# Two accumulation chains interleaved: the experts' first layer alternates between its two PSUM banks

## The chip, the cores and the metric

One core of a Trainium2 chip runs the whole kernel. The metric is device time in microseconds (us) of one execution, the median over several runs; lower is better. Busy times, waits and single instructions come from one profiled execution. Short names in the rows: PE is TensorE's matmul side, PEld its weight loads, DVE VectorE, ACT ScalarE, POOL GpSimd, SP the engine that issues most DMAs.

## What is computed

The program is one layer of a graph network over 6250 rows of 256 features. The layer norm of the rows feeds a graph part and a linear-attention part; their sum with the input is normalised again and goes through eight experts, weighted by a router. The change lies in the experts:

```
h = einsum('bfd,edh->bfeh', x, W1) + b1
h = relu(_bn(h, g1, be1, m1, v1))
h = einsum('bfeh,ehk->bfek', h, W2) + b2
h = relu(_bn(h, g2, be2, m2, v2))
y = einsum('bfeh,ehd->bfed', h, Wo) + bo
return einsum('bfed,fe->bfd', y, w)
```

## The kernel before, in words

The rows are cut into 13 chunks: chunk 0 has 240 rows, chunks 1 to 11 have 512, chunk 12 has 378. A first stage (to about 170 us) goes over all rows for the graph tables and the attention sums and loads the expert weights into SBUF. The rest of the time is a loop over chunks, and in each over the eight experts. Activations lie with features on the 128 partitions and rows along the free dimension, so 256 features are two halves of 128: an input half `k` and an output half `h`.

Every product keeps close to fp32 by splitting both factors into a high and a low part (`fp32r`) and adding three products: high times high, high times low, low times high. `mm3` issues them (lines 300, 301 and 302) for both input halves: six matmuls into one bank. A layer of an expert is two such groups, one for each output half: twelve matmuls, each 128x128 weights with `R` moving columns, where R is the chunk's number of rows.

The order is written out by hand on each engine. TensorE's loop for expert `e` issues L1 of expert e+1 (or of expert 0 of the next chunk), then L2 of e, then L3 of e-1, and after them some work for the next chunk. So three layers of other experts, 36 matmuls, stand between an expert's L1 and its L2, and as many between its L2 and its L3.

- `L1(ch, e)` writes banks 0 and 1 (`L1b[h]`). Each half waits until ScalarE has read the bank for the expert before (`r1`, counted by half) and raises `l1` when it is complete. In the first expert of a chunk it also waits for the low part of the turned input (`f2lo`, counted by input half).
- ScalarE: `relu1` does, for each half in turn, `relu` (line 960, from the bank to `activated`, raises `r1`) and `high1` (line 809, the high part, `h_high`). `relu2` does the same for the second layer: both `relu`s to `weight_stage`, then both high parts (`h`), which wait until L3 has read the only `h` buffer.
- VectorE: `hid1` takes the low parts (`h_low`, line 1403), which release L2; `weigh_hidden` (line 1548) multiplies by the router's weight; `hid2` takes the low parts of the second layer (`h`, line 1403), which release L3. Work for the next chunk stands between these, among it `route` (from line 1700) and `weights`.
- In chunk 0 TensorE also has `router_turn` (line 1339), which waits for VectorE's `weights`, and GpSimd issues two of chunk 1's gathers only when `h1` has reached 2 and 4, that is behind the first two experts' `hid1`.

Of the kernel before, what the change touches and what calls it, by code (L numbers as in the profile page):

```python
# [13 lines left out]
P = 128  # L14
KT = D // P
# [6 lines left out]
NE = 8  # L22
# [48 lines left out]
def need(eng, sem, value):  # L71
    if value > 0:
        eng.wait_ge(sem, value)
# [14 lines left out]
def build(nc, I, out):  # L88
    ctx = ExitStack()
    with ctx:  # L90
        def sb(name, shape, dt=fp32):
            return ctx.enter_context(nc.sbuf_tensor(name, shape, dt))

        def sem(name):
            return ctx.enter_context(nc.semaphore(name))
# [22 lines left out]
        xTh = sb("xT_high", [P, 2, KT, CH], f32r)  # L118
        xTl = sb("xT_low", [P, 2, KT, CH], f32r)
# [94 lines left out]
        L1b, L2b, Yb, Fb = bank[0:2], bank[2:4], bank[4:6], bank[6:8]  # L214
# [10 lines left out]
        s = {n: sem("s_" + n) for n in names}  # L225
# [66 lines left out]
        def mm3(dst, lhs, rhs, ready=None, first=True, final=True):  # L292

            last = None
            n = len(lhs)
            for k in range(n):
                (ah, al), (bh, bl) = lhs[k], rhs[k]
                if ready:
                    ready(k)
                nc.tensor.matmul(dst, ah, bh, start=(first and k == 0), stop=False)  # L300
                nc.tensor.matmul(dst, ah, bl, start=False, stop=False)  # L301
                last = nc.tensor.matmul(dst, al, bh, start=False, stop=(final and k == n - 1))  # L302
            return last
# [771 lines left out]
        def _(pe):  # L1075
# [24 lines left out]
            for k in range(KT):  # L1100
                need(pe, s["kv_w"], k + 1)
                for i in range(KT):
                    last = nc.tensor.matmul(KVb[2 + i][:, :], (centre if i == k else spread), wkv[:, k, :],  # L1103
                                            start=False, stop=(k == KT - 1))
# [3 lines left out]
            for k in range(KT):  # L1108
                last = nc.tensor.matmul(XTb[0][:, 0:D], onesf[:, :], wg[:, k, 0:D], start=(k == 0), stop=(k == KT - 1))
# [100 lines left out]
            for grp in range(2):  # L1210
                last = nc.tensor.matmul(KVb[1 - grp][:, 0:D], kvT[:, grp, :], w1m[:, grp, :], start=True, stop=True)
# [4 lines left out]
            for k in range(KT):  # L1216
                for grp in range(2):
                    last = nc.tensor.matmul(KVb[2 + k][:, 0:D], wqT[:, grp, k * P:(k + 1) * P], Pm[:, grp, :],
                                            start=False, stop=(grp == 1))
# [3 lines left out]
            for h in range(2):  # L1223
                for grp in range(2):
                    last = nc.tensor.matmul(XTb[0][:, h:h + 1], Pm[:, grp, h * P:(h + 1) * P], bqc[:, grp:grp + 1],
                                            start=(grp == 0), stop=(grp == 1))
# [3 lines left out]
            def W(layer, e, k, lo, hi):  # L1230
                m = layer * NE + e
                return whi[:, m, k * D + lo:k * D + hi], wlo[:, m, k * D + lo:k * D + hi]

            def L1(ch, e):
                R = ch.rows

                def turned(k):
                    need(pe, s["f2lo"], KT * ch.c + k + 1)

                for h in range(2):  # L1240
                    need(pe, s["r1"], 2 * NE * ch.c + 2 * (e - 1) + h + 1)
                    mm3(L1b[h][:, 0:R], [W(0, e, k, h * P, (h + 1) * P) for k in range(KT)],
                        [(xTh[:, ch.par, k, 0:R], xTl[:, ch.par, k, 0:R]) for k in range(KT)],
                        turned if e == 0 and h == 0 else None).then_inc(s["l1"], 1)

            def L2(ch, e):
                R = ch.rows
# [113 lines left out]
            idle(3)  # L1361
            pe.wait_ge(s["wst_lo"], len(JOBS))
            L1(CHUNKS[0], 0)
            router(CHUNKS[0])

            for ch in CHUNKS:
                nxt = None if ch.last else ch.next()
                for e in range(NE):
                    if e + 1 < NE:
                        L1(ch, e + 1)  # L1370
                    elif nxt is not None:
                        L1(nxt, 0)
                    L2(ch, e)
                    if ch.c == 0:
                        if e == 0:
                            router_turn(ch)
                        elif e == 1:
                            out_bias(ch)
                    if e > 0:
                        L3(ch, e - 1)  # L1380
                    elif ch.c > 0:
                        L3(ch.prev(), NE - 1)
                    if e == 2 and ch.c > 0:
                        out_bias(ch)
                    if ch.c == 0 and e == 2:
                        mix2(nxt)
                    elif nxt is not None and by_dma(nxt) and e == 5:
                        pass
                    elif nxt is not None and e in FRONT and not (ch.c == 0 and e == 3):
                        FRONT[e](nxt)  # L1390
# [429 lines left out]
```

## Time and profile before

| | |
|---|---|
| median of 3 runs | 1075.84 us (1074.94 to 1076.32) |
| profiled execution, its own time | 1074.75 us |
| its span, first to last instruction | 1072.9 us |
| matmuls | 5316, PE busy 1060.2 us |
| ScalarE busy | 727.1 us |
| VectorE busy | 774.4 us |
| mean granted TensorE clock | 0.998 |

The profiled execution took 1.85 us more than its span, and its time lies 1.09 us under the median. A matmul's length in the profile is longer than the distance to the next one's start, since matmuls overlap; the distance between starts is what a matmul costs when the stream is dense. Starts are printed to 0.01 us.

### The profile page before, as it was taken

The page shows a single profiled execution, that of the slowest core. Times are in us where ns is not written, and L with a number is a line of the kernel's source. Part 1 is how long each engine was busy: PE and PEld are TensorE (multiplying, and loading weights), DVE is VectorE, ACT ScalarE, POOL GpSimd, SP SyncE. Part 2 cuts the span into 40 slices and gives each one's busy share as a digit, 9 for nine tenths or more (in the row PEclk, how much of TensorE's full clock was granted, in tenths as well). Part 3 has the DMA queues.
Part 4 walks back from the last instruction along what each step waited for, and adds up shares of the span by engine and source line. Part 5 has one row for each costly group of instructions (what it writes and reads, how often), then busy time and mean ns, then how long its engine had stood idle before and what let it go on. Part 6 is the DMA issues. An engine that isn't in the chain of part 4 may idle for free.

```text
span 1072.9 us, 16901 instructions
## 1 busy us (share of the span) xinstructions
PE 1060.2 (99%) x5316; PEld 899.0 (84%) x5316; DVE 774.4 (72%) x1644; ACT 727.1 (68%) x1263; POOL 279.6 (26%) x308
## 2 busy tenths in 40 slices
PE   9999998999999999999999999999999999999997
PEld 7998987988888888888888888888888888888897
DVE  8888756868686686776866867768768668676664
ACT  5777756676775766757757767667667576675674
POOL 4787764303023022130130321211302202110010
PEclk9999999999999999999999999999999999999999
DMA  6877852244154244441641443325416423341030
GB/s 193 267 232 250 246 176 61 81 112 120 23 141 117 72 82 109 110 107 46 142 115 46 113 109 99 88 75 124 118 23 145 115 82 65 93 112 26 3 95 15
DMA packets 235439, 116.55 MB, mean 109 GB/s; under 512 B 170932, under 2 KB 217918, under 8 KB 235350
## 3 DMA queue, kind: packets, MB, share of 16 engines
q1 hardware_dynamic: 229070, 107.94, 37.8%
q0 software_dynamic: 3968, 6.71, 2.4%
q10 hardware_dynamic: 2311, 0.84, 0.3%
q8 instruction: 42, 0.69, 0.3%
q14 instruction: 48, 0.39, 0.1%
HBM read 77.46 MB, written 37.97 MB: 108 GB/s over the span
## 4 chain that ended last, share of the span: by engine, by line
PE 93%; DVE 2%; issue 2%; POOL 1%; DMA 1%; ACT 1%; SPq 0%; POOLq 0%; DVEq 0%; ACTq 0%
PE bank L300 29%; PE bank L301 29%; PE bank L302 29%; PE bank L1146 2%; PE bank L1333 1%; PE bank L1087 1%; PE bank L1351 1%; PE bank L1079 1%; POOL gathered L751 0%; POOL alpha_l L753 0%; PE bank L1103 0%; DMA expert_weight_rows<-expert_weights 0%; DMA expert_weights<-router_w_blocks 0%; DVE h_low L1403 0%; ACT activated L960 0%
## 5 line engine op out<-in xcount | busy, mean ns | idle before, releaser
L809 ACT ACTIVATE h<-weight_stage 128x512 fp32r<-128x512 f32 (+2 forms) x206 | 117.7, 603 | 191.5 <-PE bank L302 108.8
L1403 DVE TENSOR_TENSOR h_low<-activated,h_high 128x512 fp32r<-128x512 f32 (+2 forms) x208 | 136.3, 666 | 93.7 <-ACT h_high L809 91.2
L1403 DVE TENSOR_TENSOR h<-weight_stage,h 128x512 fp32r<-128x512 f32 (+2 forms) x206 | 126.8, 657 | 80.3 <-ACT h L809 80.3
L960 ACT ACTIVATE activated<-bank,bn_cols 128x512 f32<-128x512 f32 (+2 forms) x208 | 154.6, 743 | 39.4 <-PE bank L302 37.7
L960 ACT ACTIVATE weight_stage<-bank,bn_cols 128x512 f32<-128x512 f32 (+2 forms) x208 | 149.7, 745 | 21.6 <-PE bank L302 21.1
L300 PE MATMUL bank<-h_high,ffn_w_high 128*128 128x512 f32 (+2 forms) x420 | 158.1, 376 | 0.1
L301 PE MATMUL bank<-h_low,ffn_w_high 128*128 128x512 f32 (+2 forms) x420 | 157.8, 376 | 0.0
L302 PE MATMUL bank<-h_high,ffn_w_low 128*128 128x512 f32 (+2 forms) x420 | 157.8, 376 | 0.0
L300 PE MATMUL bank<-xT_high,ffn_w_high 128*128 128x512 f32 (+2 forms) x416 | 157.1, 378 | 0.1
L301 PE MATMUL bank<-xT_low,ffn_w_high 128*128 128x512 f32 (+2 forms) x416 | 156.7, 377 | 0.0
L302 PE MATMUL bank<-xT_high,ffn_w_low 128*128 128x512 f32 (+2 forms) x416 | 156.5, 376 | 0.0
L300 PE MATMUL bank<-h,ffn_w_high 128*128 128x512 f32 (+1 forms) x380 | 146.4, 385 | 0.9 <-DVE h L1403 0.9
L302 PE MATMUL bank<-h,ffn_w_low 128*128 128x512 f32 (+1 forms) x380 | 146.4, 385 | 0.0
L301 PE MATMUL bank<-h,ffn_w_high 128*128 128x512 f32 (+1 forms) x380 | 146.4, 385 | 0.0
L778 POOL TENSOR_TENSOR accumulated<-accumulated,normalised 128x512 f32<-128x512 f32 x22 | 37.8, 1741 | 393.2 <-DVE normalised L1557 393.2
L809 ACT ACTIVATE h_high<-activated 128x512 fp32r<-128x512 f32 (+2 forms) x208 | 126.1, 606 | 6.6
L300 PEld LDWEIGHTS bank<-h_high,ffn_w_high 128*128 128x128 f32 x420 | 78.9, 188 | 14.7 <-DVE h_low L1403 0.5
L302 PEld LDWEIGHTS bank<-h_high,ffn_w_low 128*128 128x128 f32 x420 | 79.0, 188 | 13.7
L301 PEld LDWEIGHTS bank<-h_low,ffn_w_high 128*128 128x128 f32 x420 | 78.9, 188 | 13.7
L300 PEld LDWEIGHTS bank<-xT_high,ffn_w_high 128*128 128x128 f32 x416 | 78.2, 188 | 14.0 <-issue 0.5
L302 PEld LDWEIGHTS bank<-xT_high,ffn_w_low 128*128 128x128 f32 x416 | 78.2, 188 | 14.0
L301 PEld LDWEIGHTS bank<-xT_low,ffn_w_high 128*128 128x128 f32 x416 | 78.2, 188 | 13.4
(244 smaller groups left out, 1992.8 us busy)
## 6 DMA issues: line engine op xcount, KB each, us to landing
expert_weight_rows<-expert_weights SPq DMA_DIRECT2D x44, 256.0 KB, 3.9
x_rows<-in_x SPq DMA_DIRECT2D x18, 512.0 KB, 4.8
x_turned<-xT_high SPq DMA_DIRECT2D x22, 256.0 KB, 3.4
x_turned<-xT_low SPq DMA_DIRECT2D x22, 256.0 KB, 4.6
x_rows<-accumulated SPq DMA_DIRECT2D x11, 512.0 KB
x_rows<-expert_weights SPq DMA_DIRECT2D x22, 256.0 KB, 6.0
accumulated<-x_rows SPq DMA_DIRECT2D x88, 64.0 KB
out<-accumulated SPq DMA_DIRECT2D x88, 64.0 KB, 1.9
```

Source lines behind the costliest of these rows:

```text
L300: nc.tensor.matmul(dst, ah, bh, start=(first and k == 0), stop=False)
L301: nc.tensor.matmul(dst, ah, bl, start=False, stop=False)
L302: last = nc.tensor.matmul(dst, al, bh, start=False, stop=(final and k == n - 1))
L778: nc.gpsimd.tensor_tensor(x2b[:, h, 0:w], x2b[:, h, 0:w], yblk[:, h, 0:w], ALU.add).then_inc(s["fin"], 1)
L809: return nc.scalar.activation(dst, src, ACT.Copy)
L960: nc.scalar.activation(dst[:, h, 0:ch.rows], src[h][:, 0:ch.rows], ACT.Relu, bias=bnp[:, 1, layer, col:col + 1], scale=bnp[:, 0, layer, co ...
L1079: nc.tensor.matmul(XTb[1][:, 0:P], onesf[:, :], onesf[:, :], start=True, stop=True)
L1087: last = nc.tensor.transpose(Tb[:, k, i * T.tp:(i + 1) * T.tp], xn[0:T.tp, T.slot, k * P:(k + 1) * P], ident[0:T.tp, 0:T.tp])
L1146: last = nc.tensor.matmul(Sb[:, grp * P:(grp + 1) * P], kvn[0:tp, p, vc], kvn[0:tp, p, kc], start=False, stop=final, skip_group_check=True)
L1333: last = nc.tensor.matmul(Fb[0][:, 0:ch.rows], wr4[:, i % KT, :], part, start=(i == 0), stop=(i == len(parts) - 1))
L1351: nc.tensor.matmul(Yb[h][:, 0:ch.rows], bo3[0:3 * NE, 0, h * P:(h + 1) * P], wT[:, 0:ch.rows], start=False, stop=False).then_inc(s["fbo"], 1)
L1403: return V.tensor_tensor(dst, full, high.bitcast(fp32), ALU.subtract)
```

## The change

In `L1` the two groups of six become one loop. The input half is the outer loop, the three products the middle one, and the output half the inner one. Each piece of the moving operand (high or low part of one input half) is thus streamed twice in succession, with another 128x128 weight tile and into the other bank. The order of the three products changes too: high weights with high rows, low weights with high rows, high weights with low rows. The number of matmuls and of weight loads, their shapes, and all work of the other engines stay as they are.

```
-                for h in range(2):
-                    need(pe, s["r1"], 2 * NE * ch.c + 2 * (e - 1) + h + 1)
-                    mm3(L1b[h][:, 0:R], [W(0, e, k, h * P, (h + 1) * P) for k in range(KT)],
-                        [(xTh[:, ch.par, k, 0:R], xTl[:, ch.par, k, 0:R]) for k in range(KT)],
-                        turned if e == 0 and h == 0 else None).then_inc(s["l1"], 1)
+                for k in range(KT):
+                    xh, xl = xTh[:, ch.par, k, 0:R], xTl[:, ch.par, k, 0:R]
+                    if e == 0:
+                        turned(k)
+                    for step in range(3):
+                        for h in range(2):
+                            if k == 0 and step == 0:
+                                need(pe, s["r1"], 2 * NE * ch.c + 2 * (e - 1) + h + 1)
+                            wh, wl = W(0, e, k, h * P, (h + 1) * P)
+                            last = nc.tensor.matmul(L1b[h][:, 0:R], (wh, wl, wh)[step], (xh, xh, xl)[step],
+                                                    start=(k == 0 and step == 0), stop=(k == KT - 1 and step == 2))
+                            if k == KT - 1 and step == 2:
+                                last.then_inc(s["l1"], 1)
```

TensorE's rows for L1 of expert 1 in chunk 0, before. Bank 0 and bank 1 are the two output halves; a row ends with the semaphores that the instruction waits for.

```order
L300 MATMUL bank0<-xT_high,ffn_w_high 128x240 [waits s_r1]
L301 MATMUL bank0<-xT_low,ffn_w_high 128x240
L302 MATMUL bank0<-xT_high,ffn_w_low 128x240
L300 MATMUL bank0<-xT_high,ffn_w_high 128x240
L301 MATMUL bank0<-xT_low,ffn_w_high 128x240
L302 MATMUL bank0<-xT_high,ffn_w_low 128x240
L300 MATMUL bank1<-xT_high,ffn_w_high 128x240 [waits s_r1]
L301 MATMUL bank1<-xT_low,ffn_w_high 128x240
L302 MATMUL bank1<-xT_high,ffn_w_low 128x240
L300 MATMUL bank1<-xT_high,ffn_w_high 128x240
L301 MATMUL bank1<-xT_low,ffn_w_high 128x240
L302 MATMUL bank1<-xT_high,ffn_w_low 128x240
```

Bank 0 is complete with the sixth matmul, and the second wait stands on the seventh. The same place in the changed kernel:

```order
L1249 MATMUL bank0<-xT_high,ffn_w_high 128x240 [waits s_r1]
L1249 MATMUL bank1<-xT_high,ffn_w_high 128x240 [waits s_r1]
L1249 MATMUL bank0<-xT_high,ffn_w_low 128x240
L1249 MATMUL bank1<-xT_high,ffn_w_low 128x240
L1249 MATMUL bank0<-xT_low,ffn_w_high 128x240
L1249 MATMUL bank1<-xT_low,ffn_w_high 128x240
L1249 MATMUL bank0<-xT_high,ffn_w_high 128x240
L1249 MATMUL bank1<-xT_high,ffn_w_high 128x240
L1249 MATMUL bank0<-xT_high,ffn_w_low 128x240
L1249 MATMUL bank1<-xT_high,ffn_w_low 128x240
L1249 MATMUL bank0<-xT_low,ffn_w_high 128x240
L1249 MATMUL bank1<-xT_low,ffn_w_high 128x240
```

Bank 0 is now complete with the eleventh matmul, bank 1 with the twelfth as before, and the wait for bank 1 stands on the second matmul. Every other L1 moves in the same way; in chunks 1 to 11 its rows read 128x512.

## Rows read from the trace of the kernel before

**Rows 1.** The page, part 1: busy time, share of the span, instructions

```profile
PE 1060.2 (99%) x5316; PEld 899.0 (84%) x5316; DVE 774.4 (72%) x1644; ACT 727.1 (68%) x1263; POOL 279.6 (26%) x308
```

**Rows 2.** The page, part 4: chain that ended last, by engine

```profile
PE 93%; DVE 2%; issue 2%; POOL 1%; DMA 1%; ACT 1%; SPq 0%; POOLq 0%; DVEq 0%; ACTq 0%
```

**Rows 3.** TensorE's waits from 170 us on: total us, times, longest

```profile
PE bank L1339 <- DVE router_w L1399: 1.6, 1, 1.6
...
PE bank L300 <- DVE h L1403: 1.3, 2, 0.9
```

**Rows 4.** Windows: stretch, us, busy by engine, TensorE clock, DMA share, GB/s

```profile
280.40:353.10 72.70, 72.70 (x332) 60.12 (x331) 52.72 (x104) 49.22 (x76) 14.00 (x13) 1.00 0.38 96
```

**Rows 5.** Timeline of PE, chunk 7, L1 of expert 5: start, us

```profile
693.76 0.39 PE L302 MATMUL bank<-xT_high,ffn_w_low 128*128 128x512 f32 x1
693.99 0.39 PE L300 MATMUL bank<-xT_high,ffn_w_high 128*128 128x512 f32 x1
...
695.35 0.39 PE L300 MATMUL bank<-h_high,ffn_w_high 128*128 128x512 f32 x1
...
700.79 0.39 PE L300 MATMUL bank<-xT_high,ffn_w_high 128*128 128x512 f32 x1
```

**Rows 6.** Timeline of PE in the set-up, lines 1103 and 1109

```profile
8.83 3.60 PE L1103 MATMUL bank<-activated,gathered 128*128 128x512 f32 x8
12.27 0.59 PE L1109 MATMUL bank<-weight_stage,ones 128*128 128x256 f32 x2
```

**Rows 7.** Timeline of PE, chunk 0, from L1 of expert 0

```profile
174.56 0.27 PE L302 MATMUL bank<-xT_high,ffn_w_low 128*128 128x240 f32 x1
...
175.12 0.27 PE L301 MATMUL bank<-xT_low,ffn_w_high 128*128 128x240 f32 x1
...
175.79 0.27 PE L300 MATMUL bank<-xT_high,ffn_w_high 128*128 128x240 f32 x1
...
177.37 0.38 PE L300 MATMUL bank<-h_high,ffn_w_high 128*128 128x240 f32 x1
...
180.57 0.29 PE L1339 MATMUL bank<-identity,router_w 120*64 120x120 f32 x1 [1.60 <-DVE router_w L1399]
```

**Rows 8.** Timeline of ACT, chunk 0, expert 0

```profile
174.87 0.56 ACT L960 ACTIVATE activated<-bank,bn_cols 128x240 f32<-128x240 f32 x1 [0.23 <-PE bank L302]
...
175.77 0.54 ACT L960 ACTIVATE activated<-bank,bn_cols 128x240 f32<-128x240 f32 x1
176.34 0.40 ACT L809 ACTIVATE h_high<-activated 128x240 fp32r<-128x240 f32 x1
```

**Rows 9.** Timeline of DVE, chunk 0, expert 0 and the router

```profile
176.59 0.72 DVE L1403 TENSOR_TENSOR h_low<-activated,h_high 128x240 fp32r<-128x240 f32 x2
177.23 1.02 DVE L1700 STREAM_TRANSPOSE router_w<-bank 32x64 f32<-32x64 f32 x4
```

**Rows 10.** Timeline of ACT, chunk 1, expert 2, second half

```profile
233.54 0.76 ACT L960 ACTIVATE activated<-bank,bn_cols 128x512 f32<-128x512 f32 x1
```

**Rows 11.** Timeline of PE, chunk 1, start of L1 of expert 3

```profile
233.40 0.39 PE L300 MATMUL bank<-xT_high,ffn_w_high 128*128 128x512 f32 x1
233.63 0.39 PE L301 MATMUL bank<-xT_low,ffn_w_high 128*128 128x512 f32 x1
```

**Rows 12.** Chain of work around a wait of PE: start, us, what

```profile
230.46 0.14 issue
230.59 0.47 PE bank L300
```

**Rows 13.** Timeline of ACT, chunk 7, expert 5, first half

```profile
694.19 0.78 ACT L960 ACTIVATE activated<-bank,bn_cols 128x512 f32<-128x512 f32 x1 [3.06 <-PE bank L302]
```

**Rows 14.** Chunk 9: ACT's second half of expert 0, PE's L1 of expert 1

```profile
796.29 0.77 ACT L960 ACTIVATE activated<-bank,bn_cols 128x512 f32<-128x512 f32 x1
...
798.95 0.39 PE L300 MATMUL bank<-xT_high,ffn_w_high 128*128 128x512 f32 x1
```

**Rows 15.** Timeline of ACT, chunk 12, second layer of expert 6

```profile
1060.94 0.52 ACT L809 ACTIVATE h<-weight_stage 128x378 fp32r<-128x378 f32 x1 [1.46 <-PE bank L302]
```

## The prediction, written before the changed kernel ran

> **What bounds the kernel now.** I read the busy times first: PE is busy for 99% of the span, ScalarE for 68%, VectorE for 72% [rows 1]. A busy PE alone proves little, so I read the chain of waits next: 93% of it is PE [rows 2]. The list of TensorE's waits then has only 4.4 us from 170 us on, in four waits, all at 172 to 231 us; the two groups of them that matter here are shown [rows 3]. One whole chunk of 512 rows (72.7 us) has PE busy throughout at a granted clock of 1.00 [rows 4]. So from chunk 2 on, the time is the number of matmuls times the distance between their starts, and the change can act in two ways only: by altering that distance, or by making TensorE wait where it did not.
>
> **The distance between starts.** In L1 of a chunk with 512 rows, the last six matmuls go from 693.99 to 695.35: 0.227 us each [rows 5]. 512 columns at 2.4 GHz take 0.213 us, so about 13 ns of each matmul is not streaming. If that were the price of adding twice in a row into one bank, a matmul that starts another bank would be cheaper. The trace before has such pairs: the sixth matmul of L1 ends the work on bank 0 and the seventh opens bank 1, at 693.76 and 693.99, 0.23 us apart [rows 5]. The twelfth to L2's first changes bank, rows and weights, and is no nearer. Hence I cost the alternation at nothing.
>
> The other new property, the same rows streamed twice in succession into two banks, has one likeness in the set-up: line 1103 multiplies each input half with two weight tiles into banks 2 and 3, twice over (eight records). They take (12.27 - 8.83) / 8 = 0.430 us each [rows 6]. These are plain fp32, two passes of 512 columns for each record, so 0.427 us is pure streaming. Here too a repeated stream is neither faster nor slower. I take 0.227 us after the change. The bounds are: if the whole 13 ns went away in all of L1's 1248 matmuls (13 chunks by 8 experts by 12), 16.6 us less; if a bank change cost as much again, 16.6 us more. The rows of before stand at the zero between these ends.
>
> The Trainium skill (TensorE: Matmul & The Clock Gate, the section "Wait — 56ns, not 53.3ns?") gives a warm matmul about 2.5 ns over its streaming time. This trace differs: it has 13 ns for these fp32r matmuls. If the new order brought L1 to the page's figure, an estimate from the page is 1248 x 11 ns = 14 us less; by the trace's own bank changes it is nothing.
>
> **What becomes late.** The first bank is complete with the eleventh matmul instead of the sixth: 5 x 0.227 = 1.13 us later in the large chunks, 5 x 0.112 = 0.56 us in chunk 0. The second bank is complete when it was. ScalarE's `relu` of the first half can start 0.43 us after the start of the bank's last matmul (694.19 against 693.76, [rows 5, 13]). I went along all 104 experts. In 47 ScalarE starts less than 1 us after the bank is due and shifts by most of this, up to 1.13 us; in the others it is already late with other work, and loses less or nothing. The two halves of ScalarE's work follow each other without a gap, so all of `relu1` shifts, then VectorE's `h_low`, and `relu2` behind it.
>
> In chunks 1 to 12 that lateness is covered. Between an expert's L1 and its L2 stand 36 matmuls of other layers, 36 x 0.227 = 8.2 us, and the next L1 starts 6.6 us after the `relu` that waited (694.19 to 700.79, [rows 5, 13]). The tightest release of a next L1 after chunk 1 is in chunk 9: ScalarE has read bank 1 at 796.29 + 0.77 = 797.06, the next L1 starts at 798.95, 1.89 us later [rows 14]; and there `relu` waits for the router's exponential, not for the bank, so nothing shifts. In chunk 12, with 378 columns for 512, the lateness is about 0.85 us, and ScalarE sits idle for 1.46 us before the high parts of the second layer [rows 15]. Those high parts wait for L3's reading of the `h` buffer, a TensorE time. So the end is not touched either.
>
> **Term 1, chunk 0, expert 0: +0.42 us.** Here there is no cover. `relu` starts at 174.87, 0.31 us after the sixth matmul's start at 174.56. The eleventh starts at 175.12, so it would be 175.43 [rows 7, 8]. The second half's high part goes from 176.34 to 176.90 and ends at 177.30. VectorE's second `h_low` can then start at about 177.33 and takes 0.40, to 177.73; now the pair ends at 176.59 + 0.72 = 177.31 [rows 9]. So `route` behind it is 0.42 us late, then the router's weights, for which TensorE waits 1.6 us at line 1339 [rows 3, 7], and the gathers that GpSimd issues after `h_low`. I find no slack that takes it up.
>
> **Term 2, the early wait in chunk 0: 0.** L1 of expert 1 starts at 175.79 [rows 7]. Its second matmul now needs ScalarE's second read, which ends at 175.77 + 0.54 + 0.56 = 176.87 [rows 8]. With 0.14 us from a release to the matmul (seen at 230.59, [rows 12]) it goes at 177.01, the twelfth near 178.2, and L2 at 178.3 instead of 177.37. L2 then ends at about 179.7, still before the router's release at 180.57 + 0.42. The wait of 1.6 us hides it. Were that cover gone, it would cost some 0.9 us.
>
> **Term 3, the early wait in chunk 1: +0.8 us.** L1 of expert 3 starts at 233.40 and its second matmul at 233.63 [rows 11]. ScalarE, late after the wait for the first expert weights, reads bank 1 for expert 2 only at 233.54 to 234.30 [rows 10]. Before, the wait stood on the seventh matmul (234.76) and was met. Now it stands on the second, which goes at 234.30 + 0.14 = 234.44 instead of 233.63: 0.81 us. The chain gives the first matmul after such a wait 0.47 us at 230.59 [rows 12], so some 0.1 us of restart may come on top; I leave it to the range. Behind this point PE has no wait that could absorb it. Bounds: 0 if ScalarE is earlier in another run, 1.1 us if the wake-up is slower.
>
> **Sum.** 0.42 + 0 + 0.81 = +1.2 us. Span 1072.9 becomes 1074.1; with the 1.85 us outside it, 1075.95 against the profiled 1074.75. Put on the median of the runs, 1075.84 + 1.2 = 1077.0 us, or 0.11% more. A difference under 0.2% (2.15 us) can't be told from none, so my verdict is "the same".
>
> **Rivals.**
>
> (a) The distance shrinks. For it speaks the unexplained 13 ns; against it the bank changes at full distance and the repeated streams of line 1103. Those are not the same thing as twelve alternations in fp32r, so I leave it a chance. At full effect 1077.0 - 16.6 = 1060.4 us; at a third of it 1071.5. It decides from 3 ns for each matmul on. 8%.
>
> (b) Slower through waits in every chunk. The lateness of 1.13 us also moves VectorE, and with it the turned rows of the next chunk, which travel through DRAM. If one release in each of chunks 1 to 12 ran out of slack by 0.5 us, the sum is 6 us: 1083. It decides from 0.07 us a chunk. Against it: the tightest gap that I found after chunk 1 is 1.89 us. 10%.
>
> (c) The distance grows, because two open chains or a repeated stream cost something that a single change of bank does not show. 3 ns each make 3.7 us: 1080.7. 4%.
>
> (d) The clock. L1 in one chunk with the clock at its lower level would cost 12 x 0.227 = 2.7 us for each expert. Against it: the six banks 0 to 5 are already gone through in turn at a granted clock of 1.00 [rows 4], and the only new idle time is under 1.2 us at a stretch. The Trainium skill (TensorE: Matmul & The Clock Gate, "A second HAM failure mode: psum-queue depth-cycling") says that cycling through banks can leave small idle gaps that make the clock swing. One expert's L1 at half rate is 1077.0 + 2.7 = 1079.7 us. 3%.
>
> (e) The change does as above: 75%, of which a few in a hundred fall past either bound by the scatter of the runs (the three shown span 1.4 us).
>
> **The numbers.** Faster by over 0.2% (under 1073.7): 8% from (a) and 1% of (e). Slower by over 0.2% (over 1078.0): 17% from (b), (c), (d) and 2% of (e), since my sum already leans that way. The same: 72%. The range takes in the scatter of 0.7 us to each side, both ends of term 3, and the small halves of (a) and (b): 1074.3 to 1079.3.
>
> **What the profile after would show.** The distance of L1's starts at 0.227 us. `relu` of the first half 0.43 us after the eleventh matmul. A gap of about 0.8 us beyond the usual distance between the first and second matmul of L1 of expert 3 in chunk 1, and one of about 1.1 us in expert 1 of chunk 0, with the wait at the router's turn shortened. No further TensorE waits after 240 us, and every chunk of 72.7 us. A chunk that is more than 0.1 us off that would make the prediction wrong; so would a distance other than 0.227.

## The result, and the profile after

The changed kernel takes 1077.62 us (median of 19 runs, 1076.88 to 1079.87) beside 1075.84 us for the kernel before (19 runs of the same session, 1074.44 to 1077.44). The ratio is 1.0019, with a 95% interval of 1.0012 to 1.0026, so +2.0 us (1.3 to 2.8); the two medians by themselves lie 1.78 us apart. That is just inside the 0.2% that stood for "the same". The profiled execution took 1078.52 us with a span of 1076.7 us, 3.8 us more span than before. The page after, busy times and then the chain by engine:

```profile
PE 1062.4 (99%) x5316; PEld 900.3 (84%) x5316; DVE 773.2 (72%) x1644; ACT 723.5 (67%) x1263; POOL 273.7 (25%) x308
...
PE 94%; issue 1%; POOL 1%; DVE 1%; ACT 1%; DMA 1%; SPq 0%; POOLq 0%; ACTq 0%; DVEq 0%
```

The counts are those of [rows 1], and TensorE is the chain as in [rows 2]. TensorE's waits from 170 us on (us in total, times, longest):

```profile
PE bank L1249 <- ACT activated L960: 1.6, 3, 0.6
PE bank L300 <- DVE h L1411: 1.6, 2, 1.2
PE bank L1333 <- DVE normalised L1681: 1.5, 1, 1.5
PE bank L1347 <- DVE router_w L1407: 1.2, 1, 1.2
```

The first row is new: three waits for ScalarE in the changed loop, at line 1249. The last answers to the 1.6 us at line 1339 in [rows 3] and is 0.4 us shorter. All lie ahead of 240 us. Two chunks of 512 rows, in windows as in [rows 4]:

```profile
284.50:357.23 72.73, 72.73 (x331) 60.16 (x330) 53.19 (x105) 48.98 (x76) 13.36 (x13) 1.00 0.39 96
357.23:429.96 72.73, 72.73 (x331) 60.16 (x330) 51.76 (x104) 48.70 (x76) 13.47 (x13) 1.00 0.39 97
```

TensorE is busy from end to end at a granted clock of 1.00. Measured from the first router matmul of one chunk to that of the next, each of the chunks 2 to 10 takes 72.73 us in both kernels. Inside the L1 groups of chunks 2 to 11, the mean distance between starts is 227.2 ns before and 227.2 ns after (880 distances each). TensorE's timeline at the place of [rows 5], the end of L1 of expert 5 in chunk 7 and L2's first:

```profile
698.68 0.61 PE L1249 MATMUL bank<-xT_low,ffn_w_high 128*128 128x512 f32 x2
699.13 0.39 PE L300 MATMUL bank<-h_high,ffn_w_high 128*128 128x512 f32 x1
```

The first row holds the eleventh and twelfth matmul, bank 0's last and bank 1's last. ScalarE's timeline beside it:

```profile
699.11 0.78 ACT L960 ACTIVATE activated<-bank,bn_cols 128x512 f32<-128x512 f32 x1 [4.19 <-PE bank L1249]
```

ScalarE reads bank 0 0.43 us after the eleventh matmul's start, the same delay as in [rows 5, 13] (694.19 against 693.76); its idle time ahead of that grew from 3.06 to 4.19 us, by the 1.13 us of five matmuls. None of that reaches TensorE.

So the loss lies in chunks 0 and 1. In chunk 0, ScalarE's timeline after:

```profile
176.78 0.55 ACT L960 ACTIVATE activated<-bank,bn_cols 128x240 f32<-128x240 f32 x1 [0.79 <-PE bank L1249]
177.36 0.40 ACT L809 ACTIVATE h_high<-activated 128x240 fp32r<-128x240 f32 x1
177.67 0.53 ACT L960 ACTIVATE activated<-bank,bn_cols 128x240 f32<-128x240 f32 x1
178.23 0.40 ACT L809 ACTIVATE h_high<-activated 128x240 fp32r<-128x240 f32 x1
```

VectorE's:

```profile
177.94 0.40 DVE L1411 TENSOR_TENSOR h_low<-activated,h_high 128x240 fp32r<-128x240 f32 x1
178.67 0.41 DVE L1411 TENSOR_TENSOR h_low<-activated,h_high 128x240 fp32r<-128x240 f32 x1 [0.33 <-ACT h_high L809]
179.00 1.02 DVE L1708 STREAM_TRANSPOSE router_w<-bank 32x64 f32<-32x64 f32 x4
```

And TensorE's in chunk 0, then in chunk 1 (L1 of expert 1, then of expert 3):

```profile
177.38 0.38 PE L1249 MATMUL bank<-xT_high,ffn_w_high 128*128 128x240 f32 x1
178.25 0.38 PE L1249 MATMUL bank<-xT_high,ffn_w_high 128*128 128x240 f32 x1 [0.49 <-ACT activated L960]
179.59 0.27 PE L300 MATMUL bank<-h_high,ffn_w_high 128*128 128x240 f32 x1
...
182.34 0.29 PE L1347 MATMUL bank<-identity,router_w 120*64 120x120 f32 x1 [1.25 <-DVE router_w L1407]
...
218.94 0.40 PE L1249 MATMUL bank<-xT_high,ffn_w_high 128*128 128x512 f32 x1
219.84 0.50 PE L1249 MATMUL bank<-xT_high,ffn_w_high 128*128 128x512 f32 x1 [0.51 <-ACT activated L960]
220.19 0.64 PE L1249 MATMUL bank<-xT_high,ffn_w_low 128*128 128x512 f32 x2
...
236.31 0.39 PE L1249 MATMUL bank<-xT_high,ffn_w_high 128*128 128x512 f32 x1
237.26 0.50 PE L1249 MATMUL bank<-xT_high,ffn_w_high 128*128 128x512 f32 x1 [0.56 <-ACT activated L960]
237.60 0.63 PE L1249 MATMUL bank<-xT_high,ffn_w_low 128*128 128x512 f32 x2
```

Chunk 0's first L1 matmul is at 175.27 here and at 173.92 before. TensorE's timelines, before and after:

```profile
173.92 0.35 PE L300 MATMUL bank<-xT_high,ffn_w_high 128*128 128x240 f32 x1
...
175.27 0.35 PE L1249 MATMUL bank<-xT_high,ffn_w_high 128*128 128x240 f32 x1
```

Counted from there, the router's transpose on VectorE starts at +3.73 (179.00 - 175.27) against +3.31 (177.23 - 173.92, [rows 9]), 0.42 us later, and the released router matmul at +7.07 against +6.65 (180.57 - 173.92, [rows 7]), again 0.42. Expert 1's wait in chunk 0 (178.25) ends far ahead of that and costs nothing. In chunk 1 the wait of expert 3 is the predicted one. The wait of expert 1 at 219.84 was not predicted.

The span's 3.8 us divide so. 1.35 us lie ahead of chunk 0's first L1 matmul, in code that the change does not touch. From there to the last matmul it is 893.07 us before and 895.50 after, 2.43 more: chunk 0 has 35.85 for 35.37 (+0.48), chunk 1 has 71.96 for 70.00 (+1.96), the rest is equal.

### The profile page after: what moved, and what is told of

Same layout as the page of the kernel before. It is cut to its first block, busy times and chain, and to the rows that moved or that the text cites. A ratio compares the mean times of both kernels' runs of the same rounds, so it can differ in the third digit from the quotient of the medians.

```text
span 1076.7 us, 16901 instructions
## 1 busy us (share of the span) xinstructions
PE 1062.4 (99%) x5316; PEld 900.3 (84%) x5316; DVE 773.2 (72%) x1644; ACT 723.5 (67%) x1263; POOL 273.7 (25%) x308
## 4 chain that ended last, share of the span: by engine, by line
PE 94%; issue 1%; POOL 1%; DVE 1%; ACT 1%; DMA 1%; SPq 0%; POOLq 0%; ACTq 0%; DVEq 0%
PE bank L1249 24%; PE bank L300 21%; PE bank L302 21%; PE bank L301 21%; PE bank L1146 2%; PE bank L1341 1%; PE bank L1087 1%; PE bank L1359 1%; PE bank L1079 1%; POOL gathered L751 0%; ACT activated L960 0%; POOL alpha_l L753 0%; PE bank L1103 0%; DMA expert_weight_rows<-expert_weights 0%; DMA expert_weights<-router_w_blocks 0%
## 5 line engine op out<-in xcount | busy, mean ns | idle before, releaser
L960 ACT ACTIVATE weight_stage<-bank,bn_cols 128x512 f32<-128x512 f32 (+2 forms) x208 | 143.5, 740 | 0.9 <-remote 0.4
L1249 PE MATMUL bank<-xT_high,ffn_w_high 128*128 128x512 f32 (+2 forms) x416 | 124.3, 379 | 1.8 <-ACT activated L960 1.6
L1249 PE MATMUL bank<-xT_high,ffn_w_low 128*128 128x512 f32 (+2 forms) x416 | 122.8, 376 | 0.0
L1249 PE MATMUL bank<-xT_low,ffn_w_high 128*128 128x512 f32 (+2 forms) x416 | 122.8, 376 | 0.0
L1249 PEld LDWEIGHTS bank<-xT_high,ffn_w_high 128*128 128x128 f32 x416 | 75.9, 188 | 16.2 <-ACT activated L960 2.8
```

Of the source, the lines that this page charges most:

```text
L960: nc.scalar.activation(dst[:, h, 0:ch.rows], src[h][:, 0:ch.rows], ACT.Relu, bias=bnp[:, 1, layer, col:col + 1], scale=bnp[:, 0, layer, co ...
L1249: last = nc.tensor.matmul(L1b[h][:, 0:R], (wh, wl, wh)[step], (xh, xh, xl)[step], start=(k == 0 and step == 0), stop=(k == KT - 1 and step ...
```

## The experiments

Each run has one profile. In the sessions of the experiments the kernel before has a median of 1075.00 us (beside the first four) and 1074.83 us (beside the next four). Three stretches are compared below: chunk 0 (its first router matmul to chunk 1's), chunk 1 (to chunk 2's), and chunk 1 without the distance between the two starts around the wait for the first expert's hidden layer near 230 us (line 300 waiting for `h`). That distance is 0.75 to 1.72 us, kernels of either order lie on both sides of 1.2, and it would hide effects of this size. The ratios of whole times can't tell these kernels apart: those without either loss have 1.0007 and 1.0006, those with one of them 1.0006 and 1.0012, and the intervals overlap. Where the loss sits is read from the stretches.

**The changed kernel again.** No edit; what repeats of the 2.0 us, and where?

> The changed kernel once more, for a second profile and a tighter interval. Theory (waits at the start): ratio 1.001 to 1.0025; from L1 of expert 0 in chunk 0 on, the profile is 1.3 to 2.5 us longer than before, all of it ahead of chunk 2, chunks 2 to 11 at 72.73 us each. In the first profile ScalarE stood idle for 2.1 us at 209.5 us with nothing late for it, and TensorE then waited 0.7 us in L1 of expert 1 in chunk 1. If that pause is chance, it is gone here, and the part of chunk 1 falls to about 1.1 us (expert 3's wait of 0.8 us and what follows); if the change brings it, it is there again. Rival (the first stage before 170 us got longer by 1.4 us through the change): the first L1 starts at about 175.3 us again instead of 173.9.

Measured: 1076.19 us, ratio 1.0012 (1.0003 to 1.0021); from the first L1 matmul on 894.46 us, 1.4 more than before. Chunk 0 is 35.79 us; chunk 1 without the wait near 230 us is 69.58, for 68.71 before. Every chunk from 2 on is as before. The first L1 starts at 174.76 us. Over all twelve profiles that start lies between 173.84 and 176.60 us, and it is 174.66 in the second profile of the kernel before; so nothing shows that the change made the first stage longer. Its timeline of TensorE has the wait in L1 of expert 3 again, and none in expert 1:

```profile
235.72 0.50 PE L1249 MATMUL bank<-xT_high,ffn_w_high 128*128 128x512 f32 x1 [0.53 <-ACT activated L960]
236.06 0.62 PE L1249 MATMUL bank<-xT_high,ffn_w_low 128*128 128x512 f32 x2
```

**The old order in chunks 0 and 1.** The alternation stays in chunks 2 to 12, eleven thirteenths of it:

```
+                if ch.c < 2:
+                    for h in range(2):
+                        need(pe, s["r1"], 2 * NE * ch.c + 2 * (e - 1) + h + 1)
+                        mm3(L1b[h][:, 0:R], [W(0, e, k, h * P, (h + 1) * P) for k in range(KT)],
+                            [(xTh[:, ch.par, k, 0:R], xTl[:, ch.par, k, 0:R]) for k in range(KT)],
+                            turned if e == 0 and h == 0 else None).then_inc(s["l1"], 1)
+                    return
```

> L1 alternates in chunks 2 to 12 only; chunks 0 and 1 have the old order. Theory (all of the loss is in chunks 0 and 1): ratio to before 1.0000, within 0.0007; no TensorE wait at L1. Rival (the alternation costs in every chunk by waits or distance): ratio stays near 1.0018.

Measured: 1075.31 us, ratio 1.0007 (0.9998 to 1.0016), span 1072.8. From the first L1 matmul on 892.69 us, for 893.07 before. TensorE's waits from 170 us on:

```profile
PE bank L1354 <- DVE router_w L1414: 1.6, 1, 1.6
PE bank L1340 <- DVE normalised L1688: 1.5, 1, 1.5
PE bank L300 <- DVE h L1418: 0.8, 2, 0.4
```

No wait for ScalarE's reading is left, and the router's is back at 1.6 us. So in chunks 2 to 12 the alternation costs and gives nothing in the trace. The ratio lies at the edge of what was expected, and its interval includes 1.

**The old order in chunk 1 alone** (`ch.c == 1` in the same edit).

> Alternating except in chunk 1. Theory: only term 1 is left, 0.4 to 0.5 us, ratio 1.0004; no wait at L1 of experts 1 and 3 in chunk 1. Rival (the loss is in the steady chunks or in the first stage): ratio 1.0018.

Measured: 1075.47 us, ratio 1.0006 (0.9997 to 1.0015). Chunk 0 has 35.67 us, 0.30 more than before where 0.4 to 0.5 was expected; chunk 1 without the wait near 230 us is 68.71, exactly the value before. TensorE's waits:

```profile
PE bank L1340 <- DVE normalised L1688: 1.5, 1, 1.5
PE bank L1354 <- DVE router_w L1414: 1.2, 1, 1.2
PE bank L300 <- DVE h L1418: 0.7, 2, 0.4
PE bank L1256 <- ACT activated L960: 0.5, 1, 0.5
```

The last is chunk 0's hidden wait, and the router's wait is the shorter one of 1.2 us.

**The old order in chunk 0 alone** (`ch.c == 0`).

> Alternating except in chunk 0. Theory: term 1 is gone, the early wait of expert 3 in chunk 1 is left: 0.8 to 1.1 us, ratio 1.0009; 1.5 us (1.0014) if expert 1 of chunk 1 waits as well. Rival (the loss comes from chunk 0, whose lateness is carried on into chunk 1): ratio 1.0002 or less.

Measured: 1075.99 us, ratio 1.0012 (1.0003 to 1.0021). The opposite picture: chunk 0 is 35.28 us, chunk 1 without the wait near 230 us 69.59. TensorE's timeline in chunk 1:

```profile
230.43 0.47 PE L300 MATMUL bank<-h,ffn_w_high 128*128 128x512 f32 x1 [0.55 <-DVE h L1418]
...
234.18 0.50 PE L1256 MATMUL bank<-xT_high,ffn_w_high 128*128 128x512 f32 x1 [0.55 <-ACT activated L960]
```

With TensorE held up by only 0.55 us at 230.43, the wait in expert 3 is as long as in the other kernels. Each loss is there without the other.

**Only two of the 104 L1 in the old order**, expert 0 of chunk 0 and expert 3 of chunk 1 (`(ch.c, e) in ((0, 0), (1, 3))`).

> All of the 104 groups of L1 alternate but two: expert 0 of chunk 0 and expert 3 of chunk 1 have the old order. Theory (the loss sits in these two places: the late first bank and the early wait): ratio 1.0000 to 1.0004; the stretch from router to router of chunk 0 is 35.4 us and that of chunk 1 within 0.3 us of what its wait for the expert weights (near 230 us, 0.4 to 1.2 us in the profiles so far) makes of it, with no wait at L1 of expert 3. Rival (each alternating group of chunks 0 and 1 costs a little): the loss falls by no more than a tenth, ratio 1.0011.

Measured: 1075.53 us beside 1074.83, ratio 1.0006 (0.9997 to 1.0015). Chunk 0 is 35.45, chunk 1 without the wait near 230 us 68.67. TensorE's timeline there:

```profile
231.26 0.47 PE L300 MATMUL bank<-h,ffn_w_high 128*128 128x512 f32 x1 [1.13 <-DVE h L1418]
...
234.06 0.39 PE L300 MATMUL bank<-xT_high,ffn_w_high 128*128 128x512 f32 x1
234.29 0.39 PE L301 MATMUL bank<-xT_low,ffn_w_high 128*128 128x512 f32 x1
```

The wait is gone, with 102 of 104 experts still alternating, and the stretches are back at their lengths of before: in each of the two chunks the loss hangs on one L1. The ratio of the whole time is over the 1.0004 that was expected; its interval includes 1.

**Bank 0 three matmuls ahead.** Three into bank 0, six alternating, three into bank 1, so that bank 0 is complete with the ninth and bank 1 is opened by the fourth:

```
+                order = ([(0, 0, step) for step in range(3)] +
+                         [t for step in range(3) for t in ((1, 0, step), (0, 1, step))] +
+                         [(1, 1, step) for step in range(3)])
+                for h, k, step in order:
...
+                    if k == 0 and step == 0:
+                        need(pe, s["r1"], 2 * NE * ch.c + 2 * (e - 1) + h + 1)
```

> Every L1: three products of bank 0, then six that alternate between bank 1 and bank 0, then three of bank 1. No rows stream twice in succession. Bank 0 is complete with the ninth matmul, and the second wait stands on the fourth. Theory by the same two terms: bank 0 is 3 x 0.112 = 0.34 us late in chunk 0, of which 0.14 us is idle time of VectorE that takes it up, so +0.20 us; in chunk 1 the fourth matmul of expert 3 is due at 234.08 on the clock of before and goes at 234.44, +0.36 us and 0.1 us of restart. Sum 0.6 to 0.7 us, ratio 1.0006; the gap in L1 of expert 3 is 0.6 us instead of 0.92. Rival (alternation as such costs at the start, wherever the wait stands): 1.3 us as in the changed kernel.

Measured: 1075.82 us, ratio 1.0007 (0.9998 to 1.0016). Chunk 1 without the wait near 230 us is 69.10: +0.4 for the +0.9 of the full alternation. Chunk 0 is 35.44, only +0.1 where +0.2 was expected. The distance of starts from chunk 2 on is again 227.2 ns. TensorE's timeline in L1 of expert 3:

```profile
236.25 0.39 PE L1250 MATMUL bank<-xT_low,ffn_w_high 128*128 128x512 f32 x1
236.71 0.73 PE L1250 MATMUL bank<-xT_high,ffn_w_high 128*128 128x512 f32 x2
```

The fourth matmul follows the third at 0.46 us in place of 0.23; 0.6 was expected. The loss shrinks with the number of matmuls between L1's start and the second wait. That the wait comes early is what counts here: six of the twelve matmuls still alternate.

**Bank 0 later still, 12 matmuls.** The changed kernel makes bank 0 late by five matmuls. A wait in ScalarE's `relu`, from chunk 2 on and not for expert 0, makes that twelve: it holds the read of bank 0 until the first half of L2 is through, the 18th matmul counted from L1's first, where the kernel before has the bank ready with the sixth. That is up to 12 x 0.227 = 2.72 us:

```
+                if layer == 0 and ch.c >= 2 and e > 0:
+                    need(act, s["l2"], 2 * NE * ch.c + 2 * (e - 1) + 1)
```

> The changed kernel, and from chunk 2 on ScalarE's read of the first layer waits in experts 1 to 7 for the first half of the L2 that follows on TensorE as well: bank 0 is read after the 18th matmul instead of the 11th, 2.72 us later than before the change, 2.4 times its lateness. It prices the cover. Theory (1.89 us or more of slack wherever ScalarE waits for nothing else, mostly 4): no or little loss on top of the changed kernel, at most 0.3 us a chunk; chunks 2 to 11 at 72.73 to 73.0 us; ratio 1.0012 to 1.004. Rival (the slack is used up soon after the 1.13 us of the change): over 0.5 us a chunk, ratio above 1.006.

Measured: 1076.71 us, ratio 1.0019 (1.0010 to 1.0028); the changed kernel had 1.0019 and 1.0012 in its two comparisons. Two of its chunks in windows:

```profile
283.06:355.79 72.73, 72.73 (x332) 60.17 (x330) 51.40 (x103) 48.41 (x75) 13.41 (x13) 1.00 0.38 96
355.79:428.52 72.73, 72.73 (x331) 60.17 (x330) 52.17 (x104) 48.43 (x76) 13.36 (x13) 1.00 0.38 97
```

Still 72.73 us, and no wait of TensorE after 240 us; only the end of chunk 12 is 0.3 us later. That the delay took hold is seen in chunk 7's expert 5. TensorE's timeline, L2's sixth matmul:

```profile
698.82 0.39 PE L302 MATMUL bank<-h_high,ffn_w_low 128*128 128x512 f32 x1
```

And ScalarE's:

```profile
699.30 0.78 ACT L962 ACTIVATE activated<-bank,bn_cols 128x512 f32<-128x512 f32 x1 [5.47 <-PE bank L302]
```

ScalarE reads bank 0 only behind that matmul, after 5.47 us of idle time for the 4.19 of the changed kernel and the 3.06 of [rows 13]. The cover in the large chunks is at least this big.

**Bank 0 later by 18 matmuls.** The same wait with `+ 2` in place of `+ 1`, so for both halves of L2, 4.1 us.

> As the run before, but waiting for both halves of that L2: bank 0 is read after the 24th matmul, 4.08 us later than before the change. Theory: the next L1 starts 8.2 us after this one and both reads take 2.1 us after 5.6 us, so 0.4 us is left in a plain expert and nothing where VectorE or ScalarE have work for the next chunk: waits of TensorE appear in a few experts of each chunk, 1 to 4 us a chunk, ratio 1.01 to 1.04. If the chunks stay at 72.73 us here too, the cover is larger than I read from the timeline.

Measured: 1083.12 us, ratio 1.0077 (1.0063 to 1.0090), +8.3 us. Windows of two chunks:

```profile
283.81:356.99 73.18, 73.04 (x331) 60.08 (x331) 51.28 (x103) 47.85 (x74) 12.69 (x13) 1.00 0.38 96
356.99:430.46 73.47, 73.32 (x331) 59.92 (x331) 51.91 (x104) 48.48 (x76) 12.79 (x13) 1.00 0.37 96
```

Now each chunk from 2 to 10 is 73.1 to 73.6 us, 0.4 to 0.9 more, and the last stretch is 1.5 us longer. That is less than the 1 to 4 us a chunk and the ratio of 1.01 or more that were expected: the cover was again read too small. But it has an edge, between 2.7 and 4.1 us of lateness. This is how rival (b) would have looked in a profile; nothing of it is in the changed kernel's.

**One more profile of each kernel**, before and changed.

> The kernel before once more, one look, for what varies between profiles of the same program. Expected: chunk 0 from router to router 35.37 us within 0.05; chunk 1 69.5 to 70.5 us, by its wait for the expert weights near 230 us; chunks 2 to 10 at 72.73 us; the first L1 anywhere from 173.8 to 176.6 us.

> The changed kernel a third time, one look. Theory: chunk 0 at 35.8 us; chunk 1 at 70.5 to 71.2 us, or near 72.0 us if ScalarE makes its pause near 210 us again (seen in one of two profiles of this program and perhaps in one of its kin). Rival (the pause belongs to the changed program): it is there again.

Measured: before again 1075.43 us, span 1073.6, chunk 0 at 35.34, chunk 1 without the wait near 230 us 68.74; changed again 1076.22 us (before beside it 1075.12), span 1074.4, chunk 0 at 35.72, chunk 1 likewise 69.60. With that wait, chunk 1 is 69.95 and 70.48 us, as expected to 0.02.

Sums over all profiles. Chunk 0 with expert 0 in the old order is 35.28 to 35.45 us in five kernels, before and its repeat among them (mean 35.37); with expert 0 alternating in full 35.67 to 35.85 in six (mean 35.78): +0.41. Chunk 1 without the wait near 230 us is 68.67 to 68.79 with expert 3 in the old order, in five kernels (mean 68.72). Alternating, it is 69.53 to 69.60 in four (mean 69.58), +0.85. In the two that are left, the changed kernel's first profile and the one with 12 matmuls of lateness, it is 70.38 and 70.25.

## Why the prediction was right, point by point

**The distance between starts** stayed at 227.2 ns (rivals (a) and (c) fall). Neither the alternation of banks nor the repeated stream of rows buys or costs anything that this trace can show. The prediction had closed its bounds of 16.6 us to none from a single bank change at 0.23 us; over the 80 L1 groups of chunks 2 to 11 before, that change from the sixth to the seventh matmul takes 227.0 ns. The Trainium skill (TensorE: Matmul & The Clock Gate, "Wait — 56ns, not 53.3ns?") puts a warm matmul about 2.5 ns over its streaming time; here the 13 ns stay in either order.

**What becomes late.** Bank 0 was late by five matmuls, and ScalarE waited for it 1.13 us longer in the place shown. In the chunks from 2 on that cost nothing. The argument by the next release was right, and cautious: a lateness of up to 2.72 us was covered too, and only six matmuls more took 0.4 to 0.9 us a chunk. Rival (b) was the right mechanism for a larger lateness, and falls for this one. The prediction's count of 47 experts takes the sixth matmul's start as the time when the bank is due; counted from 0.43 us behind it, when ScalarE could first read, it is 74. Nothing in the sum hangs on it.

**Term 1** was 0.42 by the rows and is 0.42 in the changed kernel's own rows, +0.41 over eleven profiles. **Term 2** was hidden as said: L2 began at 179.59, the released router matmul came at 182.34, and its wait shrank from 1.6 to 1.25 us. The gap ahead of the second matmul of expert 1 is 0.87 us, so 0.76 beyond the usual distance and not 1.1: the prediction let that L1 start on time, but its first matmul waits for ScalarE's late read of bank 0 (over at 176.78 + 0.55 = 177.33, matmul at 177.38).

**Term 3** was put at 0.81, with some 0.1 of restart left to the range. In the changed kernel the distance is 0.95 us for 0.227, +0.72, and the next one is 0.34, +0.11: 0.83 us together. Over the profiles the chunk grows by 0.85. That 0.81 comes so near is partly luck. The prediction took 0.14 us from the release to the matmul, from a wait for VectorE; here, where ScalarE releases, it is 0.05 (its read ends at 219.03 + 0.76 = 219.79, the matmul starts at 219.84, and the same holds for the wait at 237.26). The 0.09 too much stood in for the 0.11 of restart that was left out. The mechanism is as forecast, a wait that moved from the seventh matmul to the second and was met in the old place; the order with three matmuls of lead, which halved it, and the kernel with two old L1, which removed it, show that.

**The sum** of +1.2 us stands against +2.0 (1.3 to 2.8) in the main comparison, and +1.3 (0.3 to 2.3) in the repeat. The two terms as measured give 0.41 + 0.85 = 1.26 us. What the sum missed sits in the first profile of the changed kernel as a second stall in chunk 1, of 0.79 us (70.38 for a mean of 69.59 in the repeats). No term and no rival of the prediction has it. Its first condition stood in the profile before: in chunk 1, ScalarE's second read for expert 0 ended only 0.26 us ahead of L1 of expert 1 (216.08 + 0.76 = 216.84 against 217.10).

```profile
216.08 0.76 ACT L960 ACTIVATE activated<-bank,bn_cols 128x512 f32<-128x512 f32 x1
...
217.10 0.40 PE L300 MATMUL bank<-xT_high,ffn_w_high 128*128 128x512 f32 x1
```

With the wait on the second matmul, that leaves ScalarE 0.26 + 0.23 - 0.05 = 0.44 us to be late in. It was later than that, and the changed kernel's ScalarE timeline leads up to it:

```profile
211.64 0.55 ACT L960 ACTIVATE activated<-bank,bn_cols 128x240 f32<-128x240 f32 x1 [2.11 <-remote]
...
217.70 0.76 ACT L960 ACTIVATE activated<-bank,bn_cols 128x512 f32<-128x512 f32 x1
...
219.03 0.76 ACT L960 ACTIVATE activated<-bank,bn_cols 128x512 f32<-128x512 f32 x1
```

ScalarE was idle for 2.1 us before it read bank 0 of chunk 0's expert 7, although the eleventh matmul had started at 209.59. It was therefore late with expert 0 of chunk 1, whose second half it reads at 219.03, and the second matmul of expert 1's L1 had to wait until 219.84. The repeat of the same kernel has this at the same place:

```profile
209.32 0.55 ACT L960 ACTIVATE activated<-bank,bn_cols 128x240 f32<-128x240 f32 x1 [0.38 <-PE bank L1249]
```

There it is 0.4 us of idle, which is the plain wait for the bank: `relu` starts 0.32 us after the eleventh matmul's start (209.00), where [rows 7, 8] have 0.31 after the sixth. No wait comes in expert 1. The trace also records when each semaphore is raised. Eight profiles have chunk 0's expert 7 in one of the new orders; for them, at this place (us):

| kernel | ScalarE idle before `relu` | `l1` raised, after the start of bank 0's last matmul | wait in expert 1 of chunk 1 |
|---|---|---|---|
| changed, two repeats | 0.38 | 0.29 | none |
| chunk 1 old | 0.38 | 0.29 | (old order) |
| three matmuls of lead | 0.53 | 0.67 | none |
| two old L1 | 1.27 | 1.19 | none |
| 18 matmuls later (chunks 0 and 1 as changed) | 1.29 | 1.20 | none |
| 12 matmuls later (chunks 0 and 1 as changed) | 2.03 | 1.94 | yes |
| changed, first profile | 2.11 | 2.02 | yes |

With chunk 0 in the old order, in four profiles, ScalarE has no idle time there at all. So where the pause is long, the early second wait turns it into a stall of TensorE.

By these records it is TensorE's signal that came late, not its matmuls: `relu` starts 0.02 to 0.03 us after `l1` goes up each time. In the first profile of the changed kernel the four signals for the two halves of this L1 and of the L2 behind it come within 0.19 us, at 211.61 to 211.80, while the matmuls go on at 0.11 us each; VectorE's signals in that time come with the ends of its instructions. Why the signals came late is open. Some semaphore records just ahead of the pause are missing, so the trace is not whole there. Whether the new order brings this or the profiles of the old order just met none can't be told from eight against four. It is also open how much of the 2.0 us in the main comparison is this stall, and how much is the first stage, whose length differs by up to 2.8 us between profiles.

**The clock** (rival (d)) was 1.00 in every window with the bank changing at each matmul. The Trainium skill's warning (same page, "A second HAM failure mode: psum-queue depth-cycling") speaks of idle gaps between groups of matmuls; here no such gaps came after 240 us, and nothing swung.

**The chances.** The forecast "the same" held, but barely and with some luck: the median is 1077.62, over the 1077.0 predicted and inside the range, and the interval reaches past 0.2%. The direction was right. The weight on the slow side lay on rivals (b), (c) and (d), and none of them came.

## What to carry to other kernels

TensorE was full here, and reordering its matmuls changed nothing by itself. Look at what the order does to the semaphores: at which matmul each bank is complete, and at which one the wait for each bank stands. Alternating between two buffers delays the first one's completion and advances the second one's wait. The first was covered in the large chunks, where other layers' matmuls lie between production and use, up to at least 2.7 us; in chunk 0 the router waited behind it and it cost 0.4 us. The second cost where the consumer was behind, in chunk 1, and it takes away slack that absorbs an unlucky pause. For effects of 1 us, compare stretches between fixed instructions over several profiles: the spans of one kernel differed by up to 2.3 us (1074.4 to 1076.7) while a steady chunk repeated to 0.01 us.

## What the runs showed of the hardware beyond that

- The first matmul after a semaphore wait is followed by the next at 0.34 us in place of 0.227, 0.11 us of restart on top of the wait (237.26 to 237.60, 219.84 to 220.19, and 235.72 to 236.06 in the repeat). From the end of ScalarE's read to the released matmul it is 0.05 us at each of these waits; from VectorE's end to the matmul near 230 us it is 0.15 us in all profiles.
- TensorE's signal of a completed bank came 0.29 us after its last matmul's start in some executions, and up to 2.02 us after it in others, at the same instruction. The changed kernel itself had 2.02 us in one profile and 0.29 in two; its matmuls ran on at their distance meanwhile.
- The distance of 227.2 ns for 512 columns in fp32r was the same for one bank six times in a row, for three with six alternating, and for alternation at each matmul.
